# A transformer-like block on one core: fused residual add, swapped operands, softmax in halves, rows spread over slots, a constant product in PE's waits

## The reference

```
x = x + conv(ln_c(x))             # super-token attention
t = t + moe(ln(t))                # t: the 3136 pixels of an image as tokens of 96

conv: cells of 8x8 pixels (7x7 = 49 cells); sf = mean of each cell
      aff = softmax over the 9 neighbour cells of pixel . sf * 96**-0.5
      sft = sum over pixels of aff * pixel / (sum of aff)          # 49 super tokens
      8 heads of attention over the 49 super tokens, projection + bias
      pixel output = sum over the 9 neighbours of aff * output
moe:  gate = softmax(t gate_w + gate_b) over 4 experts, the best 2 kept and renormalised
      out = sum over experts of gate * (gelu(t w1 + b1) w2 + b2)   # 96 -> 384 -> 96
```

## Time and profile before

| | |
|---|---|
| median of 3 runs | 614.47 us (613.87 to 615.44) |
| profiled execution | 613.63 us |
| its span, first to last instruction | 611.8 us |
| PE busy | 540.3 us, 88% of the span |
| DVE busy | 470.8 us, 77% |
| ACT busy | 375.1 us, 61% |
| POOL busy | 61.1 us, 10% |
| mean granted TensorE clock | 0.968 of full speed |

### The profile page before, as it was taken

How to read it: one execution, slowest core, us unless ns; L and a number is a source line. 1 busy time by engine, 2 the same in 40 slices (tenths; PEclk the granted TensorE clock), 3 DMA queues, 4 the chain that set the end, 5 groups by cost and what they waited for, 6 DMA issues and landing times.

```text
span 611.8 us, 15261 instructions
## 1 busy us (share of the span) xinstructions
PE 540.3 (88%) x6544; PEld 422.0 (69%) x6544; DVE 470.8 (77%) x1014; ACT 375.1 (61%) x379; POOL 61.1 (10%) x49
## 2 busy tenths in 40 slices
PE   0859678999899988999899988999899679999996
PEld 0859566687677776777577776877677457777775
DVE  5044799678699999958599999957489999777776
ACT  0114206866886568857777468857777496777673
POOL 2000013110020012010030012010000122000000
PEclk9999999899999989899899989999899798999999
DMA  8635000200000000300000000000000000000000
GB/s 198 161 91 156 0 2 10 72 12 14 6 8 13 13 12 2 93 12 13 13 8 12 9 12 2 14 13 13 12 13 14 0 12 14 14 12 13 13 13 24
DMA packets 15593, 17.42 MB, mean 28 GB/s; under 512 B 13781, under 2 KB 13917, under 8 KB 15134
## 3 DMA queue, kind: packets, MB, share of 16 engines
q1 hardware_dynamic: 14498, 14.71, 9.7%
q10 hardware_dynamic: 1028, 1.75, 1.4%
HBM read 11.63 MB, written 4.82 MB: 27 GB/s over the span
## 4 chain that ended last, share of the span: by engine, by line
PE 59%; DVE 28%; issue 5%; ACT 4%; DMA 2%; ACTq 0%; DVEq 0%
PE ps L1119 21%; PE ps L1134 13%; DVE hl L788 7%; PE ps L1139 6%; PE ps L981 4%; PE ps L966 4%; DVE tmp L799 4%; DVE xs L700 3%; DVE st L678 3%; PE ps L1128 2%; DMA projx_sb<-projx 2%; DVE xt L672 2%; PE ps L1072 2%; PE ps L945 1%; PE ps L991 1%
## 5 line engine op out<-in xcount | busy, mean ns | idle before, releaser
L445 ACT ACTIVATE hh<-ps 128x1344 f16<-128x1344 f32 x112 | 144.6, 1291 | 99.0 <-PE ps L1119 98.1
L1119 PE MATMUL ps<-xhl,w_hi 97*128 97x448 f16 x672 | 188.2, 362 | 1.1 <-ACT xhl L414 1.1
L788 DVE TENSOR_TENSOR hl<-h,hh 128x1344 f16<-128x1344 f32 x112 | 173.6, 1550 | 9.8 <-ACT h L453 9.5
L453 ACT ACTIVATE h<-ps 128x1344 f32<-128x1344 f32 x112 | 144.2, 1287 | 0.0
L1134 PE MATMUL ps<-w_lo,hh 128*128 128x96 f16 x1344 | 133.0, 210 | 0.0
L1134 PE MATMUL ps<-w_hi,hh 128*128 128x96 f16 x1344 | 132.9, 210 | 0.0
L1134 PEld LDWEIGHTS ps<-w_lo,hh 128*128 128x128 f16 x1344 | 119.6, 100 | 7.9 <-issue 0.7
L1134 PEld LDWEIGHTS ps<-w_hi,hh 128*128 128x128 f16 x1344 | 121.0, 100 | 5.3 <-issue 0.2
L1119 PE MATMUL ps<-xhl,w_lo 97*128 97x448 f16 x336 | 120.9, 360 | 0.0
L799 DVE TENSOR_TENSOR tmp<-ps,gl 112x384 f32<-112x384 f32 x112 | 61.9, 553 | 69.1 <-PE ps L1139 68.4
L1119 PEld LDWEIGHTS ps<-xhl,w_hi 97*128 97x128 f16 x672 | 62.0, 102 | 46.9 <-issue 6.3
(11 more groups left out here) (140 smaller groups left out, 522.1 us busy)
## 6 DMA issues: line engine op xcount, KB each, us to landing
xt<-xtok SPq DMA_DIRECT2D x8, 618.6 KB, 10.3
xch<-x SPq DMA_DIRECT2D x4, 1176.0 KB, 8.1
out<-xt SPq DMA_DIRECT2D x28, 168.0 KB, 2.3
h<-w ACTq DMA_DIRECT2D x2, 576.0 KB
wqkv_sb<-wqkv ACTq DMA_DIRECT2D x1, 228.0 KB
tab<-table ACTq DMA_DIRECT2D x1, 127.5 KB, 6.0
xch<-cells ACTq DMA_DIRECT2D x1, 85.8 KB
projx_sb<-projx ACTq DMA_DIRECT2D x1, 36.4 KB, 13.6
```

The lines of the kernel that those rows point to most:

```text
L445: act.activation(hh[:, i % 3, :, 0:UT], z, ACT.Gelu, scale=1.0 / WS).then_inc(S["hh_ready"], 1)
L453: act.activation(h32[:, i % 2, :, :], z, ACT.Gelu, scale=1.0 / WS).then_inc(S["h_ready"], 1)
L788: dve.tensor_tensor(hl[:, i % 2, :, 0:UT], h32[:, i % 2, :, :], hh[:, i % 3, :, 0:UT], ALU.subtract).then_inc(S["hl_ready"], 1)
L1119: ins = pe.matmul(ps[:, CH * (i % 2) + c, 0:UT], ww[:, w0:w0 + 128], xhl[:, b % 2, half, r * UT:(r + 1) * UT], start=(n == 0), stop=(n == 2))
```

## The change

The program is the same in outline. What is changed:

- `weigh` and `tmp` go. `add_expert` is four scalar_tensor_tensor instructions, one for each tile, with the gate as a per-partition scalar; PE's bias product waits for `sum_done` in place of `y_read`.
- The gates: three `is_gt` comparisons of shifted slices into a padded tile, one subtraction, one reduction; the probabilities are not divided by their sum first.
- SF and SFT swap operands: the weights (`cellw` as 49 columns, `affr` as 81 columns in a zero-padded layout) are stationary, the 102 columns of the tokens move. A 102nd column carries minus twice the token's mean, so CEN becomes a transpose and SUP is not needed.
- The first softmax runs in halves of 16 and 12 tiles, the logits in quarters. Image 0's weights for SFT are made ahead of the normalised affinities.
- The rows 2 to 6 of `normalise`, `tokens_high` and `tokens_low` move from the end of the image before into slots 0, 4, 9, 12 and 16 of their own image (`NORMAL`), and `TABLE` is rewritten: SF in slots 1 and 2, CEN in 3, LOG in 18 to 21, pixels one to two slots earlier.
- `statistics` and `deviation` of image 2 run on DVE between the logits of image 1 and slot 0; those of image 3 in slots 5 to 12 of image 0. POOL's power goes, all deviations are DVE's.
- In the prologue PE multiplies a tile of ones (`keep_busy`): 44 matmuls of 384 columns ahead of SF of image 0, 24 ahead of CEN of image 1, 3 behind each of six small attention pieces. SF of image 1 is cut in seven and put between the pixel products.
- Three constant loads move from ACT's queue to the front of SP's; ACT loads its Exp and Gelu tables by dummy activations.

```diff
-XC = CE + 1
+XC = CE + 2
+NP = GP * GP
+QUARTER_T = (0, 8, 16, 22, T)
+NORMAL = {0: 2, 4: 3, 9: 4, 12: 5, 16: 6}
...
+        TABLE = {(1, 0): (2, "SF", 0, 0, 4), (1, 1): (2, "SF", 0, 1, 4), (2, 0): (2, "SF", 0, 2, 4),
+                 (2, 1): (2, "SF", 0, 3, 4), (3, 0): (2, "CEN", 0), (3, 1): (0, "TRN", 2),
                  (4, 0): (1, "SFT", 0, 0, 4), (4, 1): (1, "SFT", 0, 1, 4), (5, 0): (1, "SFT", 0, 2, 4),
+                 (5, 1): (1, "SFT", 0, 3, 4), (6, 0): (1, "SUPT", 0), (6, 1): (1, "AFT", 0), (7, 0): (1, "QKV", 0),
+                 (7, 1): (1, "AFT", 1), (8, 0): (1, "SCO", 0), (8, 1): (0, "TRN", 3), (9, 0): (1, "AFT", 2),
+                 (9, 1): (1, "PRT", 0), (10, 0): (1, "HEA", 0), (10, 1): (1, "AFT", 3), (11, 0): (1, "HET", 0),
+                 (11, 1): (1, "PRO", 0), (12, 0): (1, "PRO", 1), (12, 1): (0, "TRN", 4), (13, 0): (1, "PIX", 0),
+                 (14, 0): (1, "PIX", 1), (15, 0): (1, "PIX", 2), (15, 1): (0, "TRN", 5), (16, 0): (1, "PIX", 3),
+                 (17, 0): (1, "PIX", 4), (18, 0): (1, "PIX", 5), (18, 1): (2, "LOG", 0), (19, 0): (1, "PIX", 6),
+                 (19, 1): (2, "LOG", 1), (20, 0): (2, "LOG", 2), (20, 1): (0, "TRN", 6), (21, 0): (2, "LOG", 3),
+                 (24, 0): (1, "TRN", 0), (26, 0): (1, "TRN", 1)}
...
@@ block.sync
+            for dst, src, name in (
+                    (tab[:], table, "tab_in"), (gate_st[:], gate_w, "gatew_in"), (projx_sb[:], projx, "gatew_in")):
+                sp.dma_start(dst, src).then_inc(S[name], 16)
             load_tokens(0)
+            for dst, src in ((sfw[C:XR, :, :].rearrange("p r n -> p (r n)"), near), (xch[C:XR, :], cells)):
+                sp.dma_start(dst, src).then_inc(S["cells_in"], 16)
             load_channels(0)
-            sp.wait_ge(S["xch_in"], 16)
             load_tokens(1)
...
@@ block.scalar
-            tokens_high(0, 0)
-            tokens_high(0, 1)
-            gate_exponentials(0)
-            cells_centred(1)
-            tokens_turned(0, 0)
+            cells_turned(1)
+            tokens_high(0, 0)
+            gate_exponentials(0)
+            act.activation(scrap[:, 1:2], scrap[:, 0:1], ACT.Gelu)
+            tokens_turned(0, 0)
+            tokens_high(0, 1)
...
@@ block.vector
+            def affinity_weights(b, k):
+                t0, t1 = half_tiles(k)
+                dve.wait_ge(S["scale_ready"], 2 * b + k + 1)
...
+                dve.tensor_tensor(affn[:, t0:t1, :], aff[:, t0:t1, :], per_token(affs[:, 1, t0:t1], K9), ALU.mult
+                                  ).then_inc(S["aff_ready"], 1)
...
+            def gate_ranks(b):
+                g = gl[:, b % 2, :, :]
+                dve.wait_ge(S["gate_exp"], b + 1)
+                for d in range(1, E):
+                    ins = dve.tensor_tensor(gw[:, :, (d - 1) * 7 + 3:(d - 1) * 7 + 3 + E - d], g[:, :, d:E],
+                                            g[:, :, 0:E - d], ALU.is_gt)
...
-                dve.tensor_tensor(rows, rows, tmp[:, i % NTMP, :, :], ALU.add).then_inc(S["sum_done"], 1)
+                for j in range(TU):
+                    t = r * TU + j
+                    ins = dve.scalar_tensor_tensor(out=xt[:, b, t, 0:C], in0=ps[0:PT, Y, j * C:(j + 1) * C],
+                                                   scalar=gl[:, b % 2, t, e:e + 1], in1=xt[:, b, t, 0:C], op0=ALU.mult,
+                                                   op1=ALU.add)
+                ins.then_inc(S["sum_done"], 1)
...
+            statistics(1, 0, 7)
+            super_normalised(0)
             split_weights()
...
+            statistics(1, 21, T)
             projected(0, 0)
             projected(0, 1)
+            deviation(1)
             cell_weights(1)
...
             low_part(0)
-            logits(1, 0)
-            logits(1, 1)
-            affinity_peaks()
+            for k in range(4):
+                logits(1, k)
+            statistics(2, 0, T)
+            deviation(2)
...
@@ block.tensor
-                    ins = pe.matmul(o[0:C, r * G:(r + 1) * G], xt[:, b, t, 0:C], cellw[:, t, :], start=(j == 0),
-                                    stop=(j == TU - 1))
+                    ins = pe.matmul(place(v)[0:N, 0:XC], cell_weight(t), xt[:, b, t, :], start=(t == 0), stop=(t == T - 1),
+                                    skip_group_check=True)
...
-                    ins = pe.matmul(o[0:XC, c0:c0 + K9], xt[:, b, t, :], affr[:, t, :], start=False,
-                                    stop=(t == T - 1), skip_group_check=True)
+                    ins = pe.matmul(place(v)[0:NP, 0:XC], super_weight(t), xt[:, b, t, :], start=(t == 0), stop=(t == T - 1),
+                                    skip_group_check=True)
...
-                    pe.wait_ge(S["y_read"], i)
+                    pe.wait_ge(S["sum_done"], i)
...
+            def keep_busy(n):
+                for _ in range(n):
+                    pe.matmul(ps[:, IDLE, 0:TU * C], ones16[:], ones16[:, 0:C].unsqueeze(1).to_broadcast([128, TU, C]),
+                              start=True, stop=True)
...
+            keep_busy(44)
+            for v in BEFORE:
...
+                if v[1] == "PIX":
+                    side(v)
+                    side((1, "SF", 0), v[2], G)
+                elif v == (1, "CEN", 0):
+                    keep_busy(24)
+                    side(v)
+                elif v != (1, "SF", 0):
+                    side(v)
+                if v[1] in ("SUPT", "QKV", "SCO", "PRT", "HEA", "HET"):
+                    keep_busy(3)
```

More of the change, by code:

```diff
@@ L62, in constants @@
     zone = (p[:, None] // ZONE == np.arange(4)[None]).astype(np.float64)
-    e = np.arange(E)
-    below = np.tile((e[None, :] < e[:, None]).reshape(1, E * E), (128, 1))
-    rank = np.tile((e - 1.5)[None], (128, 1))
-    table = np.concatenate([np.eye(128), centre, onehot, zone, below, rank], axis=1)
+    order = np.tile(np.arange(E)[None], (128, 1))
+    table = np.concatenate([np.eye(128), centre, onehot, zone, order], axis=1)
     inner = np.zeros((GP, GP))
@@ L316, in _ @@
             affinities_low(0)
-            for r in range(G):
+            for r in range(2):
                 tokens_low(0, r)
             for b in range(B):
-                if b + 1 < B:
-                    affinities_scaled(b + 1)
-                    affinities_low(b + 1)
-                    if b + 2 < B:
-                        deviation(b + 2)
-                    for r in range(G):
-                        tokens_low(b + 1, r)
+                for slot in range(SLOTS):
+                    if slot in NORMAL:
+                        tokens_low(b, NORMAL[slot])
+                    if b + 1 < B:
+                        if slot == 2:
+                            affinities_scaled(b + 1)
+                        if slot == 3:
+                            affinities_low(b + 1)
+                        if slot in (22, 23):
+                            tokens_low(b + 1, slot - 22)
         @block.scalar
@@ L330, in _ @@
             for dst, src, name in (
-                    (tab[:], table, "tab_in"), (gate_st[:], gate_w, "gatew_in"), (projx_sb[:], projx, "gatew_in"),
-                    (sfw[C:XR, :, :].rearrange("p r n -> p (r n)"), near, "cells_in"), (xch[C:XR, :], cells, "cells_in"),
                     (wproj_sb[0:C, 0:C], wproj, "small_in"), (wproj_sb[C:CB, 0:C], bproj, "small_in"),
@@ L377, in super_turned @@
                 bank = opened((b, "SUPT", 0))
-                act.copy(sfn[:], bank[0:C, 0:N]).then_inc(S["side_act"], 1)
+                act.copy(sfn[:].rearrange("p (i j) -> p i j", j=G), bank[0:C, 0:NP].rearrange("p (i j) -> p i j", j=GP)[
+                    :, 1:G + 1, 1:G + 1]).then_inc(S["side_act"], 1)
             def attention_exponentials(b):
@@ L423, in side_read @@
                 if kind == "CEN":
[L424 removed]
+                    cells_turned(b)
                 elif kind == "AFT":
@@ L477, in _ @@
             tokens_turned(0, 1)
-            for r in range(2, G):
-                tokens_high(0, r)
             hidden_high(1)
@@ L631, in super_normalised @@
                 at.link(dve.reciprocal(srec[:, 1:2], srec[:, 1:2]))
-                dve.tensor_scalar(sftT[:], bank[0:N, 0:C], srec[:, 0:1], srec[:, 1:2], ALU.add, ALU.mult
+                dve.tensor_scalar(sftT[:], bank[0:NP, 0:C], srec[:, 0:1], srec[:, 1:2], ALU.add, ALU.mult
                                   ).then_inc(S["side_dve"], 1)
@@ L789, in low_part, with add_expert @@
                                   ).then_inc(S["hl_ready"], 1)
-            def weigh(i):
+            def add_expert(i):
                 b, slot = divmod(i, SLOTS)
@@ L921, in _ @@
-                weigh(i)
+                if b == 0 and 5 <= slot <= 11:
+                    statistics(3, 4 * (slot - 5), 4 * (slot - 4))
+                if b == 0 and slot == 12:
+                    deviation(3)
                 add_expert(i)
@@ L1080, in side @@
                 elif kind == "CEN":
-                    centre_cells(b)
+                    turn_cells(b)
```

(5 more changed lines are left out.)

485 lines of the change are left out of this document (218 added, 267 removed).

## The result

Changed kernel: 614.75 us median of 20 runs (606.57 to 618.10), beside 614.65 of 20 runs for the kernel before (612.58 to 618.73). The ratio is 0.9938, 95% interval 0.991 to 0.9965: at best 0.9% faster, where 3.8% was forecast. The profiled execution took 612.89 us, its span was 611.1. The medians lie 0.1 us apart and the ratio still says 0.6%, because it leaves out as slow the six runs of the changed kernel that lie over 1.5% above its fastest (616.46 to 618.10), and none of the kernel before. The means of all 20 are 613.65 and 615.39 us, a ratio of 0.997: whether the changed kernel is faster at all is not shown. Both kernels spread over 6 to 12 us from run to run.

A forecast was written before the change was run, and what follows sets the result against it. No engine bounds throughout: a one-engine-at-a-time prologue, DVE full in images 0 to 2, and TensorE's clock. Terms −14.7 +9.2 +0.5 −4.7 −12.7 +0.2 = −22.2 from 613.63 give 591.4, said 591; range 573 to 608.

The forecast's parts named there:

- +1.0: Prologue start: image 0's tokens come later behind three loads on SP's queue; bounds 0 to +3 us, taken +1.0.
- with the clock up 9.1 becomes 5.1: Prologue cell sums of image 0: at the high clock they shrink from 9.1 to 5.1 us, −4.0.
- The other prologue stages: After the cell sums: logits to super tokens −10.6 us, super tokens −2.4, to first pixel add +1.1, pixels +1.0.
- First slots: First expert matmul to end of slot 1: 32.2 us against 23.0, +9.2, as cell weights queue behind DVE's statistics and deviation.
- Images 0 to 2: Expert slots: image 0 (slots 2 to 27) 124.2 us, +0.5; image 1 131.8, −4.7; image 2 121.6, −12.7.
- the swap that was to be free: Cell sums with operands swapped, 102 columns moving instead of 7: the swap alone costs between −0.5 and +0.5 us.
- low clock after these, 1.3: Image 1: time lost to the low clock after PE's waits, 1.3 us of the 9.5 added to its work.
- slots 25, 26: gate comparisons behind a late low_part, 2.5: Image 1, slots 25 and 26: PE waits 2.5 us for gate comparisons queued on DVE behind a late low_part.
- Fused add: A slot's DVE work: four fused instructions near 0.26 us each, 1.04 together, no change; last two slots 0.45 more each.
- Image 3: Last image, which prepares nothing and runs PE without a gap: +0.2 us.
- the clock does not hold: Rival, chance 0.15: logits, super tokens, attention and interleaved sums stay slow, 603 us; 608 if the 44 matmuls end late.
- Slower by a dear fused add: Rival, chance 0.06: the fused add costs 0.40 us an instruction, 1.6 a slot, giving 626; decided from 0.38 each.

The follow-up runs named there:

- the kernel with four edits: Changed kernel with tokens first and constant matmuls ahead, image 2's statistics spread, gate comparisons ahead, image 3's deviation dealt out: 586.58 us, ratio 0.9499.

## Why the prediction was wrong, step by step

Forecast 591 (591.4 for the profiled execution), which took 612.89. The 21.5 us of error are, within rounding:

- **Start and clock of the cell sums, 5.5.** The sum had "+1.0" for the tokens' start; the cell sums began 2.75 later than forecast, since the second half landed at 13.66. I took the three loads ahead of them (157 KB) as 1 us and didn't ask when the last half lands. Nor has the sum a term for a wait that the change drops: image 1's tokens were issued at 4.24 and image 2's at 6.02, before that half was there, where the kernel before issued image 1's at 15.26. The runs put back the order and the wait together, so the share of each stays open. The term "with the clock up 9.1 becomes 5.1" failed for the same reason: the 44 matmuls ended at 14.32 (forecast 16.5 to 17.5), PE stood for 5.87 us, and the sums took 7.81. The run with 68 matmuls shows that 5.1 was the right price for the condition, and the run with none that nothing depended on it in the whole.
- **The other prologue stages, 3.8.** Logits start to super-token start 7.87 against 7.2 and super tokens 7.76 against 7.2: these forecasts held, because 17.8 us of softmax ladder had been the real cost; that they held at the low clock, which the first of them had not assumed, is partly luck. Up to the first pixel add 21.3 instead of 19.6, pixels 10.5 instead of 9.8; the rest to the first expert matmul 11.6 against 11.4.
- **First slots, 1.5.** 33.7 against 32.2. This term was right, and so was its cause; the run that spread the statistics took 6.5 of it away.
- **Images 0 to 2, 10.6: the step that failed most.** For image 1, three sizes: PE's work at the high clock 122.3 (measured 124.3 where the clock was 1.00; the swap that was to be free costs 0.5 of it, 5.73 us for the cell sums against 5.20 before, and the rest isn't taken apart here), waits 8.2 (measured 135.73 − 128.58 = 7.15), and "low clock after these, 1.3" (measured 128.58 − 124.32 = 4.3). The waits were forecast nearly rightly in sum; what they do to the clock was sized by a third. Over images 0 to 2 the same reckoning gives some +5 for the work, −2 for the waits and +8 for the clock, an estimate for images 0 and 2, where a slot at the low clock (9, 21) was still to be taken off the kernel with four edits. The failed term is thus "low clock after these, 1.3", with the work at the high clock behind it. Among the waits the largest is "slots 25, 26: gate comparisons behind a late low_part, 2.5", a pause of the right size (2.57); with what followed it cost 3.5 us in slot 26 of image 1 and 0.9 in slot 27, of which 1.8 is added idle time of PE (2.57 against 0.60 and 0.18) and 2.6 the same instructions at the low clock. Without it images 1 and 2 take 131.3 and 119.0, against forecasts of 131.8 and 121.6.
- **Fused add: price right, role wrong.** In a stream four take 0.91 us from start to start of the next operation, 0.23 each (forecast 0.26):

```profile
363.53 0.99 DVE L818 SCALAR_TENSOR_TENSOR xt<-ps,gl,xt 112x96 f32<-112x96 f32 x4
364.44 2.03 DVE L805 TENSOR_TENSOR hl<-h,hh 128x1344 f16<-128x1344 f32 x1
```

  The last two slots take 2.95 instead of 2.52, as forecast. "No change" holds for the changed kernel, but as a sum of +2.9 and −4.4 in image 1; once the gate comparisons are out of the way it is worth 2.0%. The Trainium skill's page "VectorE: DVE Perf Modes", section "The TRN2 errata — SBUF-src ops pay a fixed extra latency per instruction", gives (120 + 96) / 0.96 = 0.225 us as an estimate; this trace agrees.
- **Image 3**: +0.45 against the forecast +0.2; 0.2 less behind its end makes up for it.

Of the rivals, "the clock does not hold" came nearest, and for its reason; but it was priced for the prologue alone (603 to 608), while most of the clock's loss that could be won back lay in images 0 to 2. "Slower by a dear fused add" is refuted by 0.23. Missing was the rival that the experiments support: the change puts a piece of DVE work just ahead of what PE waits for next, in three places (behind image 1's logits, in slot 12, in slot 25), and a PE pause can be paid twice, once as pause and once as clock.

What stays open: why the same prologue runs 6 us longer or shorter (below), and whether slot 9's wait can be taken away rather than moved; a version with the exponential or the copy on another engine wasn't tried. Of the change's parts only the fused add and the constant matmuls were taken out singly; what the swapped operands, the halves of the softmax and the spread rows give, each for itself, is not shown.

## What to carry to other kernels

When work is spread to even out an engine, ask of each piece not whether there is room in the slot but what stands behind it in the queue, and put it where the engine waits for another: the same comparisons before the waiting instruction instead of behind it were worth 1.6%. Price a new pause of TensorE above its length: in slots 26 and 27 of image 1, 1.8 us of added idle time cost 4.4, while a pause of 2.1 us in slot 9 cost 1.6 of clock in one version and nothing in another. And constant matmuls keep the clock only if they reach to the real work without a pause; measured by the whole kernel, they may still be worth nothing.

## What the runs showed of the hardware that was not expected

- Six kernels with the same instructions up to the first expert matmul reached it between 86.85 and 92.65 us, each in its one profiled execution. In the changed kernel the clock was low from 63.3 for 6.8 us and high in most of the pixel stage; where the statistics were spread it was low from 64.6 for 20.5, through the same instructions. So a prologue edit of 2 us can't be read from one profile. That this is also the spread of 6 to 12 us between runs is likely, not shown stage by stage: in the changed kernel's 20 runs the mean granted clock was 0.943 in the two fastest (606.57 and 606.83 us) and 0.916 to 0.926 in the six above 616 us. The Trainium skill's page "TensorE: Matmul & The Clock Gate", section "What's actually happening", says that the number of slow matmuls varies from run to run with the phase of the gate at the kernel's start. These traces agree that it varies (86.85 to 92.65 us); that the phase is the reason no run here shows.
- The clock fell during logits, whose operand has 31 columns, without a pause ahead of the fall. In the kernel before, PE was busy 6.80 of 6.80 us, from 100.07 on with logits, and the clock fell at 105.2:

```profile
98.30:105.10 6.80, 6.80 (x69) 6.21 (x67) 6.18 (x13) 6.70 (x10) 3.54 (x3) 1.00 0.00 0
```

  In the changed kernel it fell at 32.6, 3.1 us into unbroken logits, and stayed low for 10.2 us with PE busy 10.19. An engine that is busy by its records isn't enough.
- From the end of slot 1 on, slots without such a pause agree to 0.02 us between executions (slot 4 of image 0 took 5.89 in every run with this code): the uncertainty of this kernel lies in its prologue, and in whether a pause trips the clock.
